# One visit of ScalarE instead of two for the Gelus of a carried expert tile

## The reference, cut to what matters

```python
e = leaky_relu(a_src[src] + a_dst[dst], 0.2)
ex = exp(e - emax[dst])
alpha = ex / denom[dst]
out = segment_sum(h[src] * alpha[:, :, None], dst)      # per edge: gather a row, weigh it, add it up
...
logits = xn @ Wr + br;  top_vals, top_idx = top_k(logits, 2)      # 8 experts, 2 for each node
h = gelu(xn @ W1[e] + b1[e]);  y_e = h @ W2[e] + b2[e]            # W1 256 x 512, W2 512 x 256
y = y + y_e * w_full[..., e, None]
```

## The kernel before

| step v | engine | work |
|---|---|---|
| 0 | PE | 4 transposes of the tile's rows into PSUM bank `ps[0]` (L527) |
| 1 | DVE | biases, gates and row numbers (L563 to L565), scaled rows back from `ps[0]` into `xeT` (L567) |
| 2, 4 | PE | first product, one half (2 chunks of 128 hidden columns) at each step, both into `ps[1]` (L538) |
| 3, 5 | ACT | two Gelus each, from `ps[1]` into `hidT` (L514) |
| 6, 7 | PE | second product, one half at each step, into `ps[2]` (L548) |
| 8 | DVE | bias and gate, `ps[2]` to the result (L575, L576) |

## Time and profile before

### The profile page before, as it was taken

The page is one execution under the profiler, slowest core; times in us unless marked ns, Lnnn a source line. Parts: engine busy times, 40 slices in busy tenths (PEclk is TensorE's granted clock), DMA queues, the critical chain, the costliest instruction groups (busy, mean ns, idle before and its releaser), DMA issues. The chain is left out here.

```text
span 2759.5 us, 54621 instructions
## 1 busy us (share of the span) xinstructions
PE 1594.8 (58%) x17401; PEld 1234.3 (45%) x17401; DVE 1567.6 (57%) x5616; ACT 709.7 (26%) x2125; POOL 1876.6 (68%) x1856
## 2 busy tenths in 40 slices
PE   6566765556665444345337655764665576315995
PEld 4344444444444333233225544553554455214884
DVE  7676766667676565455555645564565556231331
ACT  6422221122222121021114323331433343111221
POOL 2576667777777777777777777777777767553442
PEclk9677675655555555555557766775677677657997
DMA  7355556644545644544555565665556555376886
GB/s 208 101 151 151 144 149 173 184 114 140 166 129 147 158 120 108 145 117 109 148 157 147 143 162 158 162 165 156 146 166 168 161 162 144 77 160 167 209 217 180
DMA packets 274153, 418.74 MB, mean 152 GB/s; under 512 B 69816, under 2 KB 204108, under 8 KB 273616
## 3 DMA queue, kind: packets, MB, share of 16 engines
q0 software_dynamic: 99024, 246.53, 34.8%
q1 hardware_dynamic: 173360, 167.20, 20.2%
q10 hardware_dynamic: 1488, 1.57, 0.2%
HBM read 341.18 MB, written 73.83 MB: 150 GB/s over the span
## 5 line engine op out<-in xcount | busy, mean ns | idle before, releaser
L966 POOL DMA_INDIRECT region<-node_table,region x1612 | 1585.3, 983 | 622.7 <-issue 476.3
L1184 PE MATMUL ps_p<-region 128*32 128x65 f32 x12896 | 390.4, 288 | 670.2 <-DVE region L1444 669.3
L1184 PEld LDWEIGHTS ps_p<-region 128*32 128x32 f32 x12896 | 302.1, 150 | 769.6 <-DVE region L1444 762.9
L1054 ACT ACTIVATE ps_p<-region 128x16 f32<-128x16 f32 x403 | 75.6, 188 | 1261.1 <-DVE region L1438 1254.1
L1444 DVE TENSOR_TENSOR region<-region,ps_p 128x512 f32<-128x512 f32 x403 | 277.0, 687 | 134.2 <-DVE region L1428 79.4
L1166 PE MATMUL ps_s<-ident,region 128*128 128x128 f32 x403 | 165.5, 411 | 286.2 <-DVE region L1438 279.9
L1424 DVE TENSOR_SCALAR region<-drep,region 128x8 f32 x403 | 102.7, 255 | 254.0 <-issue 252.3
L1452 DVE SCALAR_TENSOR_TENSOR acc<-ps_p,region,acc 128x65 f32 x806 | 193.2, 281 | 82.8 <-issue 74.3
L1166 PEld LDWEIGHTS ps_s<-ident,region 128*128 128x128 f32 x403 | 96.1, 239 | 310.5 <-DVE region L1438 303.5
L1170 PEld LDWEIGHTS ps_s<-region 128*128 128x128 f32 x806 | 201.2, 279 | 65.2 <-issue 37.9
L1048 ACT ACTIVATE region<-ps_s 128x128 f32<-128x128 f32 x403 | 111.0, 276 | 403.5 <-PE ps_s L1166 399.0
(11 more groups left out here) (328 smaller groups left out, 2760.0 us busy)
## 6 DMA issues: line engine op xcount, KB each, us to landing
region<-in_W_dram SPq DMA_DIRECT2D x84, 512.0 KB, 4.7
region<-node_table,region POOLq DMA_INDIRECT x1612
acc<-in_W_dram SPq DMA_DIRECT2D x28, 512.0 KB
acc<-base_rows SPq DMA_DIRECT2D x14, 896.0 KB, 7.3
qkv_rows<-region SPq DMA_DIRECT2D x49, 194.0 KB, 2.2
region<-expert_in SPq DMA_DIRECT2D x28, 258.0 KB, 2.9
xe<-expert_in SPq DMA_DIRECT2D x28, 258.0 KB, 4.1
node_table<-region SPq DMA_DIRECT2D x49, 132.0 KB, 1.7
```

The source lines that it names most:

```text
L966: pool.indirect_dma_start(out=rows[:, s, j, :], out_offset=None, in_=table[:, :], in_offset=bass.IndirectOffsetOnAxis(ap=idx[:, s * SUB + ...
L1184: m = pe.matmul(ps_p[s % 2][h * WIN:(h + 1) * WIN, 0:HC], wts[:, s % 2, j, h, :], rows[:, s, j, h * HC:(h + 1) * HC], start=j == 0, stop=j ...
```

## The change

The four Gelus of a carried tile are done in one visit, step 4, in place of steps 3 and 5. The second half of the first product moves from step 4 to step 3 and writes to `ps[0]`, the bank of the transposes, instead of `ps[1]`. The transposes of the next tile therefore wait for the Gelus of the tile before (`hid_ready`) rather than for its scaled rows. `hid_ready` counts one for each tile. Nothing is computed differently.

```diff
     def scalar(act, m, v):
-        if v in (3, 5):
-            half = (v - 3) // 2
-            up_ps.wait(act, 2 * m + half + 1)
-            if m and half == 0:
+        if v == 4:
+            up_ps.wait(act, 2 * m + 2)
+            if m:
                 down_ps.wait(act, m)
-            for c in (2 * half, 2 * half + 1):
-                i = act.activation(hidT[:, c, :], ps[1][:, c % 2 * MT:(c % 2 + 1) * MT], ACT.Gelu, bias=b1s[:, m % 4, c:c + 1])
+            for c in range(FC):
+                i = act.activation(hidT[:, c, :], ps[1 - c // 2][:, c % 2 * MT:(c % 2 + 1) * MT], ACT.Gelu,
+                                   bias=b1s[:, m % 4, c:c + 1])
             i.then_inc(hid_ready.sem, 1)
...
         if v == 0:
             xe_in[s].wait(pe, 16 * (m // 2 + 1))
             if m:
-                xeT_ready.wait(pe, m)
+                hid_ready.wait(pe, m)
...
-        elif v in (2, 4):
-            half = (v - 2) // 2
+        elif v in (2, 3):
+            half = v - 2
             if half == 0:
                 xeT_ready.wait(pe, m + 1)
                 w_in[s].wait(pe, 48 * (m // 2 + 1))
-            if m or half:
-                hid_ready.wait(pe, 2 * m + half)
+            if m and half == 0:
+                hid_ready.wait(pe, m)
             for f in (2 * half, 2 * half + 1):
                 for c in range(KC):
-                    i = pe.matmul(ps[1][:, f % 2 * MT:(f % 2 + 1) * MT], w1[:, c, f * P:(f + 1) * P], xeT[:, c, :],
+                    i = pe.matmul(ps[1 - half][:, f % 2 * MT:(f % 2 + 1) * MT], w1[:, c, f * P:(f + 1) * P], xeT[:, c, :],
                                   start=c == 0, stop=c == KC - 1)
...
             if b == 0:
-                hid_ready.wait(pe, 2 * m + 2)
+                hid_ready.wait(pe, m + 1)
```

More of the change, by code:

```diff
@@ L1118, in _ @@
                     part.scalar(act, *round_at(n))
[L1119 to L1122, removed]
+                m = carry_at(n, 4)
+                if m is not None:
+                    carried.scalar(act, m, 4)
         @block.tensor
@@ L1269, in _ @@
                     part.tensor(pe, *round_at(n))
-                for v in (0, 2, 4, 6, 7):
+                for v in (0, 2, 3, 6, 7):
                     m = carry_at(n, v)
@@ L1698, in any_order_stage @@
         part = rows_part(g, g["row_sems"], ps_x)
-        sems = {n: Since(c.sem, c.base + {"up_ps": 2 * CARRIED, "hid_ready": 2 * CARRIED, "listed": EARLY - 2}.get(n, CARRIED))
+        sems = {n: Since(c.sem, c.base + {"up_ps": 2 * CARRIED, "listed": EARLY - 2}.get(n, CARRIED))
                 for n, c in e["carry_sems"].items() if n not in ("xe_in", "w_in", "sent")}
```

## The result

The changed kernel takes 2745.7 us (median of 5 runs, 2742.9 to 2749.2), the kernel before 2758.8 in the same comparison: a ratio of 0.9946 [0.9926, 0.9965], 13 us faster by the medians. The mechanism is the one forecast; the gain is larger than the 11.0 predicted. The medians alone, 0.9952, would make it 2744.8; one of the five runs before took 2768.8, the next 2760.0.

The account below looks back on a forecast made before the run. The prediction took POOL to bound the kernel, with 12.3 us of true waits in the carried rounds; less 1.3 us for late index copies, 11.0 us off 2758.0 gave 2747.0 us, range 2744.5 to 2757.

Parts of the forecast that it names:

- What bounds the kernel: Carried rounds, 1415 to 2390 us: POOL is the bound; savings on other engines give back 12.3 us at most.
- Table loads: ScalarE, carried tiles: 56 loads go, 71.8 us, worth only what POOL waits less; a 1380 ns drain left out.
- Waits that go: VectorE's waits for Exp and node logits: 18.9 us removed in round 5, 12.8 in round 4.
- The moved half product: TensorE, at its new place: the second half takes 1.89 us, not 3.76, with no wait of its own.
- The new visit: Weighing behind the single Gelu visit waits 4.4 us in a round's first tile, 1.4 in the second, 8.6 a round.
- The index copy: After the visit, feeding the gather four blocks on: 1.3 us left for what POOL may still wait.
- The sum: Carried rounds: 12.3 us of POOL's waits less 1.3 gives 11.0 us gained, from 2758.0 to 2747.0 us.
- Part of it: Rival: a new wait of about 2.5 us a tile, POOL keeps about 6; 2752 us, chance 0.15.
- the waits only change place: Rival: the second half product runs at 3.76 us, new wait 3.3 a tile; 2758 us, chance 0.15.
- slower: Rival: cold matmuls and a late index copy, 4.3 us of wait a tile, 21.5 a round; 2769 us, chance 0.06.
- ScalarE is the path: Rival: all 71.8 us of ScalarE's table loads come off the time; 2686 us, chance 0.02.

Follow-up runs that it names:

- e16: Changed kernel plus a visit of one unread one-column Gelu at step 1 (56 more table loads); 2747.8 us, ratio 0.9969 to the kernel before.
- e13: Changed kernel as it is, run again beside a kernel before of 2756.1 us; 2745.4 us, ratio 0.9957.
- e14: Changed kernel with the rows' four long VectorE operations cut in seven pieces each; 2727.0 us, ratio 0.9889 to the kernel before.
- e1: Kernel before with the second half product moved to step 3 and `ps[0]`, two Gelu visits at steps 3 and 4; 2750.5 us, ratio 0.9967.
- e2: Kernel before with one Gelu visit at step 5, the second half product left at step 4 but in `ps[2]`; 2747.3 us, ratio 0.9963.
- e3: Changed kernel with Identity in place of Gelu in the carried tiles; 2746.6 us, ratio 0.9958 to the kernel before.
- e4: Kernel before with Identity in place of Gelu in the carried tiles; 2747.8 us, ratio 0.9965.
- e11: Kernel before with the carried tile's last two VectorE operations reading at most one SBUF input; 3167.5 us, ratio 1.000 to a kernel before of 3167.2.
- e15: Changed kernel with the rows' long operations in pieces and the carried tile's last operations with one SBUF input; 2725.1 us, ratio 0.9879.
- e9: Changed kernel as it is, run again beside a kernel before of 3167.2 us; 3173.4 us, ratio 1.0009.

## Why the prediction had the mechanism right and the sum too small

**What bounds the kernel.** Right. POOL is the bound of the carried rounds, and its 12.3 us of true waits were all that the chain could give back. The last stages moved up by 17 us and kept their length within 1.3.

**Table loads.** Right: 28 and 32 are left, and their 71.8 us are worth only what POOL waits less. e16 shows it from the other side. No drain is to be seen either: the Gelus start at 2204.83, where the load of 1.28 that began at 2203.53 ends, and the visit takes 4.3 us, not 7.1.

**Waits that go.** Right in kind. VectorE's waits for node logits up to 2321 us of round 5, 4.8 us in four places, are gone from the list of its waits. Over the four rounds 2.5 of 14.0 us are left, 2.06 of them at 2334.0.

**The moved half product.** Right: 1.99 us for 1.89, and 1.89 to 2.00 in 25 tiles of 28.

**The new visit.** Right for the first tile (4.4 said, 4.82 seen), half as much for the second (1.4 said, 0.67 seen). I let the mask copy ahead of the visit come after the weighing; it comes 0.69 us before it (2203.24 and 2203.93), so the visit is over earlier. Round 5 has three waits with 6.5 us where I had 8.6, and round 4 two with 3.8. Over all four rounds they are 21.0 where I had said some 30.

**The index copy.** The first of two terms of the sum that failed. I left 1.3 us for gathers whose indices come late; POOL's idle time is 197.8 against a constant of 197.6. Nothing waits for the copy: a visit of 4.3 us sits inside the lead of four blocks.

**The sum.** This is the step that failed: 11.0 said; the waits alone gave 12.1, and POOL's own instructions gave more on top. I held their busy time fixed, without a reason, and it fell: the gathers by 4.6 us from 1415 us to the end of the loop in the changed kernel's trace, by 4.1 in e13's (the sends grew by 0.8). Most of it is a changed meeting of gathers with VectorE's two-input operations. What gathers take over 0.95 us each fell in these rounds from 14.2 to 12.1 us under the rows' four long ones and from 3.5 to 1.9 under the tile's last, and e14 shows that held time counts in full. How much is the change and how much is chance of these executions stays open, since there is one trace of before: its gathers take 636.1 us in these rounds, those of after, e1, e2, e3, e4, e13 and e16 631.4 to 633.6. With the two terms as measured, 1.1 us more for the index copy and 3.8 for POOL's own instructions, the sum is 15.9 us and the time 2742.1, against 2743.1 by the ratio and 2744.8 by the medians.

Against medians the gain was 13.2 us and, in e13, 10.7; the prediction lies between the two. The range had its low end at 2744.5, 2.5 us below the time expected, which left no room for shorter gathers. By e13's ratio the time is 0.9957 x 2758.0 = 2746.1, inside the range.

**The rivals.** "Part of it" (2752), "the waits only change place" (2758) and "slower" (2769) each needed a new wait of 2.5 us or more a tile; only the first tiles have it. "ScalarE is the path" fell with e3.

## What to carry to other kernels

When one engine runs ahead of the others by some blocks and sets the pace, count its true waits, idle time less the constant of its instruction: that is all that a quicker chain on the other engines can give back, and where a stall stands matters more than how much of it there is. Then look at the bounding engine's own instructions, the long ones above all, and at what ran beside each: here 18 us lay there, more than in its waits of the carried rounds, and cutting the neighbour's long operation in pieces brought them. Ask also whether the bound is the same in every run: the same change was worth 0.4 to 0.5% in two groups and cost 0.1% in two.

## What the runs showed of the hardware

- A gather of POOL that starts under a VectorE operation with two inputs in SBUF ends 0.81 to 0.84 us after that operation: 2.01 us instead of 0.95 under one of 2.02 us. In seven pieces the same work holds them for 3.4 us in all (e14) where the whole operations held them for 22.1 (e13), for 0.48 us more of VectorE an operation. Under an operation with one of its inputs in PSUM no gather took over 1.1 us (e11, e15, and L575 in all traces).
- TensorE can take its instructions in bits with no wait that the profile names: a block's 32 matmuls then spread over up to 12.9 us instead of 1.1, in 149 blocks of 403 in e9 and in none in e13, and the same kernel takes 3173 us instead of 2745.
- An added 56 table loads of 1.283 us, at a step where ScalarE has time, moved the median by 2.4 us, within the two intervals.
